# An AdaLN transformer block: when weights are loaded and gated, who sums the rotated halves, and how the row maxima reach the heads

## The reference

```
sa, ca, ga, sb, cb, gb = silu(c) @ wmod            # per batch; ga, gb with a least size of 0.25
h = layernorm(x) * (1 + ca) + sa
q, k, v = split(h @ W_qkv.T);  q, k = rope(q), rope(k)      # rope: t * cos + rotated(t) * sin
p = softmax(causal(q @ k.T / sqrt(32)));  y = p @ v
x = x + ga * (y @ W_o.T)
h = layernorm(x) * (1 + cb) + sb
x = x + gb * moe(h)            # sigmoid gate, the best 2 of 16, W1 -> silu -> W2
```

## Time and profile before

| | us |
|---|---|
| median of 3 runs | 1663.24 |
| lowest, highest | 1660.96, 1666.24 |
| the profiled execution | 1664.53 |
| its span | 1662.6 |
| lies around the span | 1.9 |
| mean granted clock of TensorE | 0.939 of 2.4 GHz |

### The profile page before, as it was taken

The page is one execution under the profiler, slowest core; times in us unless marked ns, Lnnn a source line. Parts: engine busy times, 40 slices in busy tenths (PEclk is TensorE's granted clock), DMA queues, the critical chain, the costliest instruction groups (busy, mean ns, idle before and its releaser), DMA issues. The chain is left out here.

```text
span 1662.6 us, 27877 instructions
## 1 busy us (share of the span) xinstructions
PE 1417.6 (85%) x8713; PEld 1008.2 (61%) x8713; DVE 1252.3 (75%) x2928; ACT 832.3 (50%) x1414; POOL 726.1 (44%) x683
## 2 busy tenths in 40 slices
PE   5579998799999889999988999999783999999900
PEld 3556665566566556656655565664341899999800
DVE  3578788687778868777886777888658677777778
ACT  4324557534454753445466434546323566666622
POOL 3244445342434534243443424344524677777500
PEclk9899999999999999999999999999885999999955
DMA  6644453544344353434445353434654555445389
GB/s 218 173 152 153 134 146 89 165 121 153 101 134 137 99 165 120 153 102 133 126 109 165 114 159 94 123 94 140 214 176 154 164 173 182 158 148 169 120 324 370
DMA packets 130098, 254.56 MB, mean 153 GB/s; under 512 B 15792, under 2 KB 67504, under 8 KB 129984
## 3 DMA queue, kind: packets, MB, share of 16 engines
q1 hardware_dynamic: 101888, 177.12, 34.5%
q0 software_dynamic: 13792, 47.72, 8.5%
q10 hardware_dynamic: 14304, 28.32, 5.1%
HBM read 167.34 MB, written 85.75 MB: 152 GB/s over the span
## 5 line engine op out<-in xcount | busy, mean ns | idle before, releaser
L674 ACT ACTIVATE probs<-ring 128x1024 f32<-128x1024 f32 (+3 forms) x384 | 310.2, 811 | 191.6 <-PE ring L528 115.8
L493 PE MATMUL ring<-stack_t 96*128 96x512 f32 (+3 forms) x768 | 296.6, 410 | 26.7 <-DMA stack_t<-stack_dram 23.5
L471 PE MATMUL ring<-w_parts,h_hi 128*128 128x384 f32 x1024 | 273.8, 349 | 9.2 <-DVE neg_max L855 4.0
L858 DVE CUSTOM_DVE_ANT_0 ring<-ring,later_b 128x384 f32<-128x384 f32 (+3 forms) x512 | 247.7, 496 | 31.5 <-PE ring L493 30.3
L493 PEld LDWEIGHTS ring<-stack_t 96*128 96x128 f32 x768 | 141.8, 193 | 181.5 <-issue 66.6
L1155 POOL TENSOR_TENSOR rope_a<-rope_a,rope_b 128x256 f32<-128x256 f32 x128 | 93.2, 728 | 348.6 <-DVE rope_b L928 348.5
L1142 POOL TENSOR_TENSOR prob_sum<-prob_sum,probs 128x1024 f32<-128x1024 f32 (+3 forms) x128 | 226.1, 1766 | 28.8 <-ACT probs L674 27.7
L522 PE MATMUL ring<-stack_t 128*128 128x512 f32 (+3 forms) x768 | 212.0, 358 | 23.0 <-ACT probs L674 11.2
L471 PEld LDWEIGHTS ring<-w_parts,h_hi 128*128 128x128 f32 x1024 | 188.9, 195 | 17.9 <-issue 12.9
L855 DVE TENSOR_REDUCE neg_max<-ring 128x1 f32<-128x512 f32 x256 | 174.9, 683 | 24.8 <-PE ring L493 22.6
L471 PE MATMUL ring<-w_parts,h_lo 128*128 128x384 f32 x512 | 176.2, 344 | 0.0
(11 more groups left out here) (192 smaller groups left out, 2439.3 us busy)
## 6 DMA issues: line engine op xcount, KB each, us to landing
stack_t<-stack_dram SPq DMA_DIRECT2D x384, 128.0 KB, 3.3
stack_dram<-parts SPq DMA_DIRECT2D x64, 512.0 KB, 2.7
w_parts<-w_dram SPq DMA_DIRECT2D x24, 768.0 KB, 6.6
w_sb<-y_dram SPq DMA_DIRECT2D x32, 512.0 KB, 6.7
w_sb<-w SPq DMA_DIRECT2D x22, 512.0 KB, 5.9
x_in<-x SPq DMA_DIRECT2D x32, 256.0 KB, 3.6
x<-x SPq DMA_DIRECT2D x32, 256.0 KB, 3.6
x_dram<-x SPq DMA_DIRECT2D x32, 256.0 KB, 2.4
```

The lines of the kernel that those rows point to most:

```text
L471: mm = nc.tensor.matmul(ring[:, BANK[use], 0:384], lhs[:, c, cols], rhs[:, c, :], start=(k == 0), stop=(k == len(products) - 1))
L493: nc.tensor.matmul(ring[:, BANK[use], 0:width], stack_t[0:MROW, i % 2, 0, h, qt * P:qt * P + P], stack_t[0:MROW, i % 2, 1, h, kc * 512:kc ...
L674: nc.scalar.activation(probs[:, step % PROBS, :, q0:QC], ring[:, bank:bank + 2, q0:QC], ACT.Exp)\
L858: nc.vector.tensor_tensor_reduce(ring[:, BANK[use], 0:width], ring[:, BANK[use], 0:width], later_b[:, QC - width:QC], -1.0, 3e38, ALU.add, ...
```

## The change

The loads and gates of w_out and the loads of mod_b's rows move from the last group of a batch to its second (steps 10 to 23). The split weights come in eight transfers, one per step, that begin twelve steps ahead. From the second batch on, x is loaded five steps before its statistics. ACT writes the maxima's rows for one head, and a new transfer on SP copies them to the three others. DVE adds the two rotated halves itself, directly behind its products. Besides, in the reciprocal deviations on POOL semaphores are merged (not shown; same instructions, same waits).

```diff
-LOAD_X = {step - 2: bt for step, bt in NORM_A.items()}
-LOAD_W = {project_step(i, 0) - 10: i for i in range(G, GROUPS)}
-LOAD_MOD2 = {STEPS * (G * b + G - 1): b for b in range(B)}
-LOAD_W_OUT = {step + 2 + n: (b, n) for step, b in LOAD_MOD2.items() for n in range(G)}
-LOAD_MOD_ROWS = {step + 7: b for step, b in LOAD_MOD2.items()}
-GATE_OUT = {step + at: (b, n) for step, b in LOAD_MOD2.items() for n, at in enumerate((7, 8, 9, 11))}
+LOAD_X = {step - (5 if bt[0] else 2): bt for step, bt in NORM_A.items()}
+LOAD_W = {project_step(i, 0) - 12 + n: (i, n % 2, n // 2) for i in range(G, GROUPS) for n in range(2 * C)}
+LOAD_MOD2 = {STEPS * (G * b + 1) + 10: b for b in range(B)}
+LOAD_W_OUT = {step + n: (b, n) for step, b in LOAD_MOD2.items() for n in range(G)}
+LOAD_MOD_ROWS = {step + 5: b for step, b in LOAD_MOD2.items()}
+GATE_OUT = {step + at: (b, n) for step, b in LOAD_MOD2.items() for n, at in enumerate((7, 9, 11, 13))}
...
 @block.sync
-                    def load_w(i):
-                        if i == G:
+                    def load_w(i, k, c):
+                        if i == G and k == c == 0:
...
                         sp.wait_ge(qkv_ps, NT * (i - 1))
-                        for k in range(2):
-                            sp.dma_start(w_parts[:, i % 2, k, :, :].bitcast(f32), w_dram[k, i % G, :, :, :])\
-                                .then_inc(w_parts_in[i % 2], 16)
+                        sp.dma_start(w_parts[:, i % 2, k, c, :].bitcast(f32), w_dram[k, i % G, :, c, :])\
+                            .then_inc(w_parts_in[i % 2], 16)
...
+                    def rows_to_heads(i, half):
+                        rows = stack_t[MROW:MROW + 2 * HG, i % 2, 0, :, half * QC:half * QC + QC].bitcast(f32)
+                        sp.wait_ge(max_in, 2 * i + half + 1)
+                        sp.dma_start(rows[:, 1:HG, :], rows[:, 0:1, :].to_broadcast([2 * HG, HG - 1, QC]))\
+                            .then_inc(rows_in[half], 16)
...
                         if step in STACK_IN:
                             stack_parts(*STACK_IN[step])
+                        if step in MAX_TURN:
+                            rows_to_heads(*MAX_TURN[step])
...
 @block.tensor, project and score_columns
-                            pe.wait_ge(w_parts_in[i % 2], 32 * (i // 2 - 1))
+                            pe.wait_ge(w_parts_in[i % 2], 32 * C * (i // 2 - 1))
...
                         if kt == 0 and hp == 0:
-                            pe.wait_ge(max_in, 2 * i + qc + 1)
+                            pe.wait_ge(rows_in[qc], 16 * (i + 1))
...
 @block.scalar, rows_of_max
-                        nc.scalar.copy(stack_t[MROW:MROW + 2 * HG, i % 2, 0, :, half * QC:half * QC + QC],
-                                       row.unsqueeze(1).to_broadcast([2 * HG, HG, QC])).then_inc(max_in, 1)
+                        nc.scalar.copy(stack_t[MROW:MROW + 2 * HG, i % 2, 0, 0, half * QC:half * QC + QC], row)\
+                            .then_inc(max_in, 1)
...
 @block.vector, rope, behind its three products
+                        dve.wait_ge(rope_terms, 3 * (u + 1))
+                        nc.vector.tensor_tensor(rope_a[:, t % 2, :], rope_a[:, t % 2, :], rope_b[:, :], ALU.add)\
+                            .then_inc(roped, 1)
...
 @block.gpsimd
-                    def rope_sum(i, t):
-                        u = NT * i + t
-                        pool.wait_ge(rope_terms, 3 * (u + 1))
-                        nc.gpsimd.tensor_tensor(rope_a[:, t % 2, :], rope_a[:, t % 2, :], rope_b[:, :], ALU.add)\
-                            .then_inc(roped, 1)
...
-                        if step in PROJECT:
-                            rope_sum(*PROJECT[step])
```

More of the change, by code:

```diff
@@ L297, in adaln_block @@
             x_in_s = [sem(f"x_in{k}") for k in range(3)]
-            stat_step, rstd_step, rstd_pow, rstd_ready = (
-                sem("stat_step"), sem("rstd_step"), sem("rstd_pow"), sem("rstd_ready"))
+            stat_step, rstd_step, rstd_ready = (
+                sem("stat_step"), sem("rstd_step"), sem("rstd_ready"))
             stat_ready, x_hat_ready, h_scaled = sem("stat_ready"), sem("x_hat_ready"), sem("h_scaled")
@@ L305, in adaln_block @@
             s_ps, s_max, max_ps, max_in = sem("s_ps"), sem("s_max"), sem("max_ps"), sem("max_in")
+            rows_in = [sem("rows_in0"), sem("rows_in1")]
             neg_all_ready, parts_of_max = sem("neg_all_ready"), sem("parts_of_max")
@@ L312, in adaln_block @@
             o_ps, x1_ready, res_in = sem("o_ps"), sem("x1_ready"), [sem("res_in0"), sem("res_in1")]
-            stat2_step, stat2_ready, rstd2_step, rstd2_ready = (
-                sem("stat2_step"), sem("stat2_ready"), sem("rstd2_step"), sem("rstd2_ready"))
+            stat2_step, stat2_ready, rstd2_ready = (
+                sem("stat2_step"), sem("stat2_ready"), sem("rstd2_ready"))
             x_hat2, h2_ready = sem("x_hat2"), sem("h2_ready")
@@ L400, in _ @@
                         if step in LOAD_W:
-                            load_w(LOAD_W[step])
+                            load_w(*LOAD_W[step])
                         if step in LOAD_RES:
@@ L965, in second_statistics @@
                         if u >= 2:
-                            dve.wait_ge(rstd2_ready, u - 1)
+                            dve.wait_ge(rstd2_ready, 2 * (u - 1))
                         nc.vector.bn_stats(stats2[:, u % 2, :], x1[:, u % 2, :]).then_inc(stat2_step, 1)
@@ L981, in second_normalise @@
                                                        op0=ALU.subtract, op1=ALU.mult).then_inc(x_hat2, 1)
-                        dve.wait_ge(rstd2_ready, u + 1)
+                        dve.wait_ge(rstd2_ready, 2 * u + 2)
                         dve.wait_ge(x_hat2, u + 1)
@@ L1108, in first_deviation @@
                             .then_inc(rstd_step, 1)
-                        pool.wait_ge(rstd_step, u + 1)
+                        pool.wait_ge(rstd_step, 2 * u + 1)
                         nc.gpsimd.tensor_tensor(rstd[:, u % 2, 1:2], rstd[:, u % 2, 0:1], neg_half[:, :], ALU.pow)\
-                            .then_inc(rstd_pow, 1)
-                        pool.wait_ge(rstd_pow, u + 1)
+                            .then_inc(rstd_step, 1)
+                        pool.wait_ge(rstd_step, 2 * u + 2)
                         nc.gpsimd.tensor_scalar(rstd[:, u % 2, 2:3], mean_var[:, u % 2, 0:1], rstd[:, u % 2, 1:2], -1.0,
@@ L1119, in second_deviation @@
                         nc.gpsimd.tensor_scalar(rstd2[:, u % 2, 0:1], mean_var2[:, u % 2, 1:2], EPS, None, ALU.add)\
-                            .then_inc(rstd2_step, 1)
-                        pool.wait_ge(rstd2_step, u + 1)
+                            .then_inc(rstd2_ready, 1)
+                        pool.wait_ge(rstd2_ready, 2 * u + 1)
                         nc.gpsimd.tensor_tensor(rstd2[:, u % 2, 1:2], rstd2[:, u % 2, 0:1], neg_half[:, :], ALU.pow)\
```

## The result

The changed kernel takes **1686.2 us** (median of 4 runs, 1677.5 to 1693.4) beside 1662.4 of the kernel before on the same chip (4 runs): a ratio of 1.0137, 95% interval 1.0086 to 1.0189. It is 24 us slower, where 20 us faster was forecast. The profiled execution is the quickest of the four, 1677.5 us with a span of 1675.7, beside 1664.5 us and a span of 1662.6 before, so the two traces show only 13 of the 24 us.

A forecast was written before the change was run, and what follows sets the result against it. PE was taken to bound plain stretches of the attention phase, with time open around changes of batch. The terms -10 - 15 - 11 + 6 + 13 - 3 = -20 us gave a forecast of 1644 us, range 1625 to 1664.

The forecast's parts named there:

- The late gate: Last batch, before the out projection: PE's 8.0 us wait for POOL's gated w_out and 2.0 of clock go, minus 10.0.
- the spread transfers: Three changes of batch: moving loads away ends PE's stalls for stack_t and the clock lost behind them, minus 15.
- The sum on DVE: Rotated halves, 128 times: sooner sum minus 11, DVE's added work plus 6, waiting behind POOL's sums plus 13.
- DVE's own time: The 128 moved sums add 58 us to DVE; a tenth of it was taken to reach PE, plus 6.
- Sums held by POOL: One rope sum in four meets a running POOL sum and loses 0.88 us; 28 us of DVE, at 0.46 plus 13.
- The sooner hand-over: At the turn of the rotated halves, DVE's sum would end 0.36 us sooner than POOL's, minus 11.
- (c): POOL, rid of the rope sums, finishes its own before DVE comes, so nothing blocks: 13 us better, 1631; chance 0.20.
- The maxima's rows: ACT is rid of 42 us over 32 copies, the transfer is hidden, and probabilities are handed over sooner: minus 3.
- (a): DVE becomes the bound wherever a tile is projected, deciding from a share of 0.45 on: 1678; chance 0.10.
- (b): The stack comes late because DVE writes its parts late, so the 15 us don't come: 1659; chance 0.14.
- named for being right: No out-projection wait for POOL, score rows' wait some 15, turn's some 13, full clock from 324, sum's mean near 0.64 us.
- signs for being wrong: PE's waits for DVE's banks above 40 us, waits for the rows' transfer, stack_t stalls, or DVE sum at plain 0.42.

The follow-up runs named there:

- gate_alone: Kernel before with only the loads of w_out and mod_b and the gates moved to the batch's second group: 1643.6 us, ratio 0.9868.
- undo_gate: Changed kernel with w_out and mod_b loaded and w_out gated in the batch's last group again: 1692.1 us, ratio 1.0160 to the kernel before.
- reduce_only: undo_sum plus, in the sum's place on DVE, an equally long maximum with one SBUF input and unused result: 1661.6 us.
- sum_from_psum: Changed kernel with the first product written back to its PSUM bank, so the sum has one PSUM and one SBUF input: 1675.2 us.
- pool_paced: Changed kernel with POOL waiting, where its own rope sum used to be, for DVE's sum of that tile, without added work: 1661.3 us.
- gate_paced: gate_sum with POOL waiting for each tile's DVE sum where its own used to stand: 1659.2 us, ratio 0.9969 to the kernel before.
- undo_sum: Changed kernel with the sum of the rotated halves back on POOL: 1651.4 us, ratio 0.9913 to the kernel before.
- rows_full: gate_rows with ACT writing the maxima's rows for all four heads again ahead of the transfer: 1641.4 us.
- gate_rows: gate_alone with the maxima's rows copied by a transfer on SP and the merged semaphores: 1652.5 us.
- gate_sum: gate_alone with the sum of the rotated halves on DVE added: 1691.0 us, ratio 1.0151 to the kernel before.

## Why the prediction was wrong, point by point

**The late gate and the spread transfers, minus 10 and minus 15: right in mechanism, somewhat large.** gate_alone has both but the pieces and gains 20; with them 22 to 24, against 25. All stalls named in rows 4 and 5 are gone, also from the changed kernel, and the clock at 324 us is back at full in gate_alone. In the changed kernel it is 0.86 there. But 20 us is what the early gate is worth without the sum on DVE; taken out of the changed kernel it is worth 6 (undo_gate).

**The sum on DVE, plus 8 in all (minus 11, plus 6, plus 13): measured plus 35. This is the step that failed.** Its terms one by one:
- DVE's own time: plus 6 forecast, plus 10 measured by reduce_only. The share was 0.19, not 0.10.
- Sums held by POOL: 27 of 128 were held, 21% where 25% was forecast, but each lost 0.42 us and not 0.88, 11.4 us in all and not 28. The held sums met POOL's instruction late in its run more often than half of the way through. The price, plus 13 forecast, is 11 by sum_from_psum, with the looseness said there. That it comes near is luck: the time that DVE loses was more than twice too high, and what a lost microsecond costs PE then was too low, by these figures nearly 1 and not 0.46. The rows that gave 0.46 count the stops alone; behind the stop of 1.68 us another 3.4 us went in clock (the stretches from 292 to 300: 4 x 0.38 and 4 x 0.47), behind its like at 888 us 1.7, at 590 us none.
- The sooner hand-over: the turn's wait did shrink by 8.6 us, as said. But pool_paced and reduce_only, one with the sooner hand-over and one without, take the same time, so it seems that none of that reached the end (the two differ in more than the hand-over); what stands in its place in the changed kernel are waits for the maxima (line 530 for DVE's 866 now 10.3 us, 479 for 863 7.4) and for h (8.3).
- **What was missing: POOL's pace.** I took POOL's sums of probabilities to lie as in the trace of before. They lay so because the rope sum, waiting for DVE's products, held each one back until DVE was through with its own. Rid of it, POOL runs one sum behind the other without a break whenever ACT is ahead. 25 of the 35 us hang on that (pool_paced), 32 of 47 in gate_paced; most of the 11 us of the held sums must be among them, since only 6 of the 27 are left. By which path the rest reaches PE isn't shown: in sum_from_psum POOL runs as free (207.8 us idle before its sums, until ACT) and holds no rope sum, and it is still 14 us slower than pool_paced, but some of that may be the bank that it gives back later. The added wait also holds POOL's other work, as below, and no run parts that from its sums. The text had the release of POOL as rival (c), and as a gain of 13 us. It had asked only whether POOL would be out of the way of the rope sum, not what POOL would begin the sooner. The Trainium skill ("SBUF — State Buffer", section "Who interferes with whom") had more to say here. The rows show 1.19 and 3.23 us for sums that take 0.42 and 1.22 alone. By the Trainium skill's rule there the later of the two waits, so every wait taken from POOL's queue is a chance more for POOL to be the earlier one; the experiments with the pace agree.

One more effect of the same kind is visible once. POOL writes w_dram, 2 transfers of 768 KB by their shapes. After the change it issues them at 184.88 us, ahead of the six stack_t pieces that SP issues from 187.25; these take 4.83 us to issue and PE stalls 2.86 us at 196.90. In undo_sum the rope sum holds them until 189.74, behind the six, which take 2.68, and there is no stall. pool_paced issues them at 189.46, amid the pieces; these take 2.69 to issue there, and PE stalls 2.60 us all the same. That it is the write which delays the pieces' landing is argued from these times, not tested by itself, and the slow issue isn't needed for the stall.

**The maxima's rows, minus 3: wrong in sign where it can be seen.** ACT got rid of 40 us as worked out, and the transfer is hidden as worked out (rows_full). But the hand-over of probabilities did not come sooner: 18.6 us of waiting instead of 11.2, and 9 us more time on gate_alone. Why is open.

**The rivals.** (a), 1678, comes nearest in time, and by its own count it is past the share of 0.45 from which it decides: the sum's 35 us are 0.53 of the 65.7 us that it takes on DVE. But DVE's load isn't the cause: with the wait on POOL the sum takes 57.3 us and costs 10, a share of 0.17, and unblocked work on DVE cost 0.19. In the plain stretch PE stays at 38.9. (b) fell: no stall for stack_t is left at a change of batch. (c) fell with its sign turned.

**The signs.** Of those named for being right, line 570's wait is gone, the stack's is at 18.9 us with 15.2 of it before 80 us, the turn's is at 15.5 and DVE's; the sum's mean was 513 ns and not 640, and the clock from 324 us 0.86 and not full. None of the signs for being wrong showed: PE's waits for the banks of the maxima and of line 936 are some 34 us, under the 40 named, and no other of them is there. None of these signs looked at POOL's queue.

So the steps read: minus 20 (gate and loads), plus 9 (rows, gate_rows), minus 1 (pieces: undo_sum against gate_rows), plus 35 (sum on DVE) = plus 23. That this meets the 24 measured proves nothing: each step starts from the kernel of the last, so they must add up. The parts aren't independent: the gate is worth 20 us alone and 6 in the changed kernel, the sum costs 47 on gate_alone and 35 behind the others, the rows cost 9 on gate_alone and nothing in the changed kernel. The medians come from different chips and are each good to some 3 us. What stands in every pairing is that the sum on DVE costs most, and that the pace gives two thirds and more of it back.

## What to carry to other kernels

A wait that an engine keeps for a piece of work is also what paces the rest of its queue: before work is moved off an engine, ask what that engine will start sooner, and into whose reads it will then run. Here a bare wait in the freed engine's queue gave back 25 of 35 us, and 32 of 47. Where the neighbour can't be held back, an input in PSUM kept the VectorE sum from being held at all (424 ns), though the kernel as a whole gained only some 11 us by it.

## What the runs showed of the hardware

- A VectorE sum over 128x256 with both inputs in SBUF took 0.42 us alone and up to 1.26 us while a GpSimd sum ran (2.09 in gate_sum). With one input in PSUM its mean over 128 was 424 ns and its longest 425, in a kernel where POOL's sums start freely (sum_from_psum). A reduction over one of the SBUF tiles had a mean of 420 ns and a longest of 422, in a kernel where POOL is paced as before (reduce_only).
- Whether GpSimd is slowed by VectorE's sums can't be told from the means of its own: 1766 ns before, 1825 with the rope sums on DVE, 1792 with one of their inputs in PSUM, but 1831 in reduce_only, where the rope sums are POOL's:
```profile
L1155 POOL TENSOR_TENSOR prob_sum<-prob_sum,probs 128x1024 f32<-128x1024 f32 (+3 forms) x128 | 234.3, 1831 | 26.9 <-ACT probs L684 26.4
```
- TensorE's clock was granted at 0.62 and 0.53 of full speed over the eight us behind a stop of 1.68 us, at 0.78 and 0.79 behind one of 1.67 and at 1.00 behind one of 1.65, each at the same place of its batch; it stayed full behind one of 0.91 at the first place. So the clock lost behind such a stop was 3.4, 1.7 and 0 us: the stop's length alone didn't set it.
